# One in three of the streamed pieces of the selection stage moved from GpSimd to the vector engine

## Chip, cores and metric

One core of one Trainium2 chip. The metric is the device time of one execution in microseconds (us). The engines are named as the profile names them: PE (TensorE matmul), PEld (its weight load), DVE (VectorE), ACT (ScalarE), POOL (GpSimd) and SP (SyncE, which here only issues DMAs).

## What is computed

Four residual layers act on x of shape (8, 256, 256, 64): `x = x + layer(_gn(x))`, where `_gn` normalises each group of channels. The change lies in the last layer, a coherent semantic attention on the 512-feature view of the tensor. Here `_gn(x)` is the group norm (mean and 1/std for each image and channel), the feature rows hold 4096 points, of which 1024 are masked and 3072 are context:

```
cos  = einsum('bcm,bcn->bmn', msk_n, ctx_n)      # unit vectors, 1024 x 3072 for each image
maxc = cos.max(axis=-1);  amax = cos.argmax(axis=-1)
best = take_along_axis(ctx.transpose(0, 2, 1), amax[..., None], axis=1)
...                                               # a sequential scan blends best with its neighbours
out  = feats.at[:, :, mask_point_idx].set(gen)
```

The points occupy the first 64 of the 256 columns w of the picture. The other columns hold no points: there the layer gives back its own input, so the output is `x + _gn(x)`, which the kernel computes as `x * (1 + r) - r * mean` with r = 1/std.

## The kernel before

The program is a row of stages with a barrier between them; each is one function with hand-written programs for the five engines and semaphores between them. `select_points` (L1716) is the stage of the change. `point_rows` runs just before it and `coherent_scan` just after it.

**The selection.** For each of the 8 images b: POOL gathers 32 tiles of 128 point rows with indirect DMAs (`gather_rows`, L1801), one image ahead; ACT squares them, stores the context rows to DRAM (`cx`, L1845) and normalises them (L1854); PE transposes the tiles and DVE copies them out of PSUM (L1972). Then follow 8 search tiles. For each, PE makes 6 chunks of 128x512 cosines, ACT copies them from PSUM to one of two buffers `cos[:, i % 2]` (L1889), and DVE finds the greatest value and its place (`max` and `max_index`, L1977 and L1978; together one *search*). After the eighth DVE writes the indices `bi` (L1987, semaphore `s_bi`), and POOL gathers the best rows by them (L1832). ACT scales these in `scale_best`, which it does behind the second tile of the *next* image. ACT also does the squares of the next image behind tiles 2 to 4 and its normalising behind tiles 5 to 7; DVE does `norms` (four short instructions, L1958 to L1963) behind tile 4 and its own new work, if any, in the order in which the program lists it.

**The pointless columns.** They are cut into pieces of 128x1024 elements (512 KB). Of these the stage before does a few, and `select_points` streams 18 for each image (`NPC`) through a ring of four buffers `xt`. POOL's `stream(b)` first makes `s1` = 1 + r and `s0` = r * mean for the image (L1811, L1812, semaphore `s_sc`) and then does two `tensor_tensor` for each piece: times `s1` (L1817) and minus `s0` (L1819), both with both inputs in SBUF.

**The order of the ring.** SP issues, in this order and one after another: the load of piece n (L1785), which waits until the store of piece n-4 has landed, then the store of piece n-2 (L1780), which waits until that piece is computed. So a piece that is late holds back all later loads and stores.

**The order on POOL.** `gather_rows(0)`; then for each image b: `gather_rows(b + 1)`, `stream(b)`, wait for `s_bi` of image b, gather of the best rows of b. The last image has no `gather_rows`.

Of the kernel before, what the change touches and what calls it, by code (L numbers as in the profile page):

```python
# [10 lines left out]
ALU = mybir.AluOpType  # L11
# [15 lines left out]
PIECE = 16  # L27
# [45 lines left out]
def forward_modes(nc, tag, B, x, fa, fb, pair, eye, modes, nm, out_scale, split_rows):  # L73
# [4 lines left out]
    WG = W // G  # L78
    NPC = 8
    WP = WG // NPC  # L80
    CK = WP * C // 512
    NY = NPC * CK
    XB = 4
# [8 lines left out]
    with ExitStack() as ctx:  # L92
# [29 lines left out]
        s_pe, s_sp = m.sem("pe"), m.sem("spn")  # L122
        xv = x.rearrange("b (q p) (g t v) c -> b t p q g (v c)", p=P, g=G, t=NPC)
        fbank = [tz[0], tz[1], zp[0], zp[1]]
        with nc.Block() as block:

            @block.sync
            def _(sp):
# [5 lines left out]
                with sp.Fori(0, B) as b:  # L134
                    for i in range(NPC):
                        sp.wait_ge(s_y, b * NY + (i + 1) * CK)
                        sp.sem_inc(s_sp, 1)
                        sp.wait_ge(s_sq, b * NPC + (i + 1))
                        sp.sem_inc(s_sp, 1)
# [711 lines left out]
def spread(ap, dims):  # L851

    return bass.AP(ap.tensor, ap.offset, [[0, P]] + dims)
# [862 lines left out]
def select_points(nc, B, ft, mask_idx, ctx_idx, eye, cx, mnt, mbt, mx, x3, stats, out):  # L1716
# [9 lines left out]
    W0 = NPTS // C + EARLY * PIECE  # L1726
    NR = (W - W0) // PIECE
    NPC = 2 * NR
    with ExitStack() as ctx:
        m = Mem(nc, ctx, "sp")  # L1730
        rows = m.sb("rows", [P, 2, NT, H])
# [12 lines left out]
        xt = m.sb("xt", [P, 4, PIECE * C])  # L1744
        srow = m.sb("srow", [P, B, 2, C])
        s1, s0 = m.sb("s1", [P, PIECE, C]), m.sb("s0", [P, PIECE, C])
# [9 lines left out]
        s_sq, s_root, s_rn, s_nrm = m.sem("sq"), m.sem("root"), m.sem("rn"), m.sem("nrm")  # L1756
        s_t, s_te, s_c, s_ce = m.sem("t"), m.sem("te"), m.sem("c"), m.sem("ce")
        s_top, s_bi, s_ch, s_g2, s_mbs = m.sem("top"), m.sem("bi"), m.sem("ch"), m.sem("g2"), m.sem("mbs")
        s_row, s_sc, s_mul, s_out = m.sem("row"), m.sem("sc"), m.sem("mul"), m.sem("out")
        s_xt = [m.sem(f"xt{j}") for j in range(4)]  # L1760
        s_xs = [m.sem(f"xs{j}") for j in range(4)]

        def piece(t, n):

            b, r, i = n // NPC, n % NPC // NR, n % NR
            return t[b, r * P:(r + 1) * P, W0 + i * PIECE:W0 + (i + 1) * PIECE, :].rearrange("p w c -> p (w c)")

        ftf = ft.rearrange("b n h -> (b n) h")
        with nc.Block() as block:

            @block.sync
            def _(sp):
                sp.dma_start(idn[:, :], eye).then_inc(s_const, 16)
                sp.dma_start(idx0[:, 0:TM], mask_idx.rearrange("(t p) -> p t", p=P), allow_slow_non_contiguous=True).then_inc(s_const, 16)
                sp.dma_start(idx0[:, TM:NT], ctx_idx.rearrange("(t p) -> p t", p=P), allow_slow_non_contiguous=True).then_inc(s_const, 16)
                sp.dma_start(srow[:, :, :, :].rearrange("p b q c -> p (b q c)"), spread(stats, [[1, B * 2 * C]])).then_inc(s_row, 16)

                def store(n):
                    sp.wait_ge(s_out, n + 1)
                    sp.dma_start(piece(out, n), xt[:, n % 4, :]).then_inc(s_xs[n % 4], 16)  # L1780

                for n in range(B * NPC):
                    if n >= 4:
                        sp.wait_ge(s_xs[n % 4], 16 * (n // 4))
                    sp.dma_start(xt[:, n % 4, :], piece(x3, n)).then_inc(s_xt[n % 4], 16)  # L1785
                    if n >= 2:
                        store(n - 2)
                for n in range(B * NPC - 2, B * NPC):
                    store(n)
                for j in range(4):  # L1790
                    sp.wait_ge(s_xs[j], 16 * len(range(j, B * NPC, 4)))

            @block.gpsimd
            def _(pool):
                def gather_rows(b):
                    if b >= 2:
                        pool.wait_ge(s_cx[b % 2], 16 * (b // 2))
                        pool.wait_ge(s_nrm, b - 1)
                    pool.wait_ge(s_idx, b + 1)
                    for i in range(NT):  # L1800
                        pool.indirect_dma_start(rows[:, b % 2, i, :], None, ftf,  # L1801
                                                bass.IndirectOffsetOnAxis(ap=idx[:, i:i + 1], axis=0)).then_inc(s_g[b % 2][i // KC], 16)

                def stream(b):
                    r, mean = srow[:, b, 1, :], srow[:, b, 0, :]
                    rb = bass.AP(r.tensor, r.offset, [r.ap[0], [0, PIECE], r.ap[1]])
                    mb_ = bass.AP(mean.tensor, mean.offset, [mean.ap[0], [0, PIECE], mean.ap[1]])

                    if b:
                        pool.wait_ge(s_out, b * NPC)  # L1810
                    nc.gpsimd.tensor_scalar(s1[:, :, :], rb, 1.0, None, ALU.add)  # L1811
                    nc.gpsimd.tensor_tensor(s0[:, :, :], rb, mb_, ALU.mult).then_inc(s_sc, 1)  # L1812
                    pool.wait_ge(s_sc, b + 1)
                    for n in range(b * NPC, (b + 1) * NPC):
                        pool.wait_ge(s_xt[n % 4], 16 * (n // 4 + 1))
                        v = xt[:, n % 4, :]
                        nc.gpsimd.tensor_tensor(v, v, s1[:, :, :].rearrange("p w c -> p (w c)"), ALU.mult).then_inc(s_mul, 1)  # L1817
                        pool.wait_ge(s_mul, n + 1)
                        nc.gpsimd.tensor_tensor(v, v, s0[:, :, :].rearrange("p w c -> p (w c)"), ALU.subtract).then_inc(s_out, 1)  # L1819

                gather_rows(0)
                pool.wait_ge(s_row, 16)
                for b in range(B):
                    if b + 1 < B:
                        gather_rows(b + 1)
                    stream(b)
                    pool.wait_ge(s_bi, b + 1)
                    pool.wait_ge(s_cx[b % 2], 16 * (b // 2 + 1))
                    if b:
                        pool.wait_ge(s_bp, 4 * b)  # L1830
                    for i in range(TM):
                        pool.indirect_dma_start(best[:, i, :], None, cx[b],  # L1832
                                                bass.IndirectOffsetOnAxis(ap=bi[:, i:i + 1], axis=0)).then_inc(s_g2, 16)
# [115 lines left out]
            @block.vector  # L1949
            def _(dve):  # L1950
                ch = Chain(dve, s_ch)
                dve.wait_ge(s_const, 48)
                ch.step(nc.vector.tensor_copy(idxf[:, :], idx0[:, :]))
                nc.vector.tensor_copy(idx[:, :], idxf[:, :]).then_inc(s_idx, 1)  # L1954

                def norms(b):
                    dve.wait_ge(s_root, b + 1)
                    ch.step(nc.vector.tensor_scalar(rn[:, :], rn[:, :], CSA_EPS, None, ALU.add))  # L1958
                    nc.vector.reciprocal(rn[:, :], rn[:, :]).then_inc(s_rn, 1)
                    if b + 1 < B:  # L1960

                        ch.step(nc.vector.tensor_scalar(idxf[:, :], idxf[:, :], float(NPTS), None, ALU.add))
                        nc.vector.tensor_copy(idx[:, :], idxf[:, :]).then_inc(s_idx, 1)  # L1963

                norms(0)
                for b in range(B):
                    for i in range(NT // 2):
                        n = b * (NT // 2) + i
                        dve.wait_ge(s_t, n + 1)
                        if i == 0 and b:  # L1970
                            dve.wait_ge(s_mn, 16 * b)
                        nc.vector.tensor_copy(tc[:, :, 2 * i * P:(2 * i + 2) * P].rearrange("p r (q n) -> p q r n", q=2),  # L1972
                                              tp[n % 2][:, :, :, :]).then_inc(s_te, 1)
                    for i in range(TM):
                        n = b * TM + i
                        dve.wait_ge(s_ce, (n + 1) * NCH)
                        ch.step(nc.vector.max(top[:, i, :], cos[:, i % 2, :]))  # L1977
                        nc.vector.max_index(topi[:, i, :], top[:, i, :], cos[:, i % 2, :]).then_inc(s_top, 1)  # L1978
                        if i == SQ + 2 and b + 1 < B:
                            norms(b + 1)  # L1980
                    dve.wait_ge(s_top, (b + 1) * TM)
                    if b:
                        dve.wait_ge(s_mx, 16 * b)
                        dve.wait_ge(s_mbs, b)
                    ch.step(nc.vector.tensor_copy(bf[:, :], topi[:, :, 0]))
                    nc.vector.tensor_copy(mxo[:, :], top[:, :, 0])
                    nc.vector.tensor_copy(bi[:, :], bf[:, :]).then_inc(s_bi, 1)  # L1987
# [1144 lines left out]
```

## Time and profile before

| | |
|---|---|
| time before | 14682.73 us, median of 3 runs (14680.42 to 14685.68) |
| the profiled execution | 14687.5 us |
| its span, first to last instruction | 14685.3 us |
| busy in the span: PE / DVE / ACT / POOL | 10796.8 / 8873.9 / 6706.6 / 5138.0 us |
| `select_points`, by its first and the next stage's first DMA issue | 11450.8 to 12608.3 us |

The profile is of one execution; its rows give starts and durations in us from the first instruction. A line number is that of the kernel before. "Idle before" names what ended an engine's wait, as far as semaphore events show it. Shares of the whole span mix stages with different limits, so the rows below are taken from the stage of the change, and a few from other stages where the same kind of instruction runs under other conditions.

### The profile page before, as it was taken

What the parts mean: (1) busy time and instruction counts of PE and PEld (TensorE: products, weight loads), DVE (VectorE), ACT (ScalarE), POOL (GpSimd) and SP (SyncE); (2) the same over time, 40 slices, a digit from 0 to 9 for tenths busy, and PEclk for the clock granted to TensorE, in tenths of its full rate; (3) what the DMA queues carried; (4) which work ended last, traced back from release to release, by engine and by line L of the source; (5) the groups of instructions that cost most, each with busy time, mean ns of one, the idle gap of its engine ahead of it and who ended that gap; (6) DMA issues with size and microseconds to landing.
All of it is one profiled execution on the core that took longest, in us unless ns stands there. A gap on an engine that the chain in (4) does not pass through costs nothing. (4 is left out here: it accounts for less than half of the span.)

```text
span 14685.3 us, 297339 instructions
## 1 busy us (share of the span) xinstructions
PE 10796.8 (74%) x113226; PEld 7857.0 (54%) x113226; DVE 8873.9 (60%) x20267; ACT 6706.6 (46%) x10775; POOL 5138.0 (35%) x3844
## 2 busy tenths in 40 slices
PE   8655665999999999787787879986774677454432
PEld 3243222777777777666666668852322333344432
DVE  3213444777777777788888843322544545599992
ACT  5311222777777777566666632245233444222220
POOL 0002443656555655433333345520000689200001
PEclk9878887999999999999999989998787888555555
DMA  6686775111111111111111159997899666300008
GB/s 261 186 183 187 241 234 188 40 40 43 40 43 40 43 40 41 47 46 70 47 54 62 47 209 363 363 327 257 315 377 384 234 200 221 86 25 23 18 10 324
DMA packets 1298491, 2188.40 MB, mean 149 GB/s; under 512 B 116749, under 2 KB 951069, under 8 KB 1231781
## 3 DMA queue, kind: packets, MB, share of 16 engines
q1 hardware_dynamic: 878084, 1649.47, 33.9%
q10 hardware_dynamic: 398624, 463.54, 8.9%
q0 software_dynamic: 20608, 58.22, 1.4%
q8 instruction: 921, 15.09, 0.4%
q14 instruction: 254, 2.07, 0.0%
HBM read 1371.45 MB, written 799.58 MB: 148 GB/s over the span
## 5 line engine op out<-in xcount | busy, mean ns | idle before, releaser
L781 POOL TENSOR_TENSOR la_s<-la_s,la_mx 128x512 f32<-128x512 f32 x2048 | 2093.2, 1043 | 1458.0 <-DVE la_mx L740 1457.6
L820 ACT ACTIVATE la_et<-la_pt 128x512 f32<-128x512 f32 x2048 | 1120.2, 598 | 723.4 <-PE la_pt L652 723.4
L652 PE MATMUL la_pt<-la_idn,la_s 128*128 128x128 f32 x8192 | 1174.4, 289 | 214.8 <-POOL la_s L781 214.3
L740 DVE TENSOR_REDUCE la_mx<-la_s 128x16 f32<-128x1024 f32 x1024 | 1243.0, 1214 | 17.7
L732 DVE TENSOR_TENSOR la_s<-la_ps,la_post 128x2048 f32<-128x2048 f32 x512 | 1167.5, 2280 | 25.1 <-PE la_ps L638 25.1
L652 PEld LDWEIGHTS la_pt<-la_idn,la_s 128*128 128x128 f32 x8192 | 921.6, 146 | 328.1 <-issue 224.2
L2252 ACT ACTIVATE cs_sm<-cs_sm,cs_gq,cs_tt 8x1 f32<-8x1 f32 x1024 | 395.0, 386 | 1187.6 <-DVE cs_sm L2336 1187.6
L2135 PE MATMUL cs_tb<-cs_tt,cs_sel 8*128 8x16 f32 x2048 | 448.2, 370 | 652.6 <-DVE cs_tt L2334 652.6
L1439 PE MATMUL pj_pp<-pj_pw,pj_at 128*128 128x256 f32 x4096 | 927.5, 380 | 0.0
L956 PE MATMUL gm_xp<-gm_fws,gm_y 128*128 128x258 f32 x2048 | 561.6, 421 | 421.7 <-ACT gm_ri L1040 421.7
L1439 PEld LDWEIGHTS pj_pp<-pj_pw,pj_at 128*128 128x128 f32 x4096 | 759.3, 190 | 92.9
L1942 PE MATMUL sp_cp<-sp_tc 128*128 128x512 f32 x1536 | 694.8, 612 | 155.2 <-ACT sp_cos L1889 149.0
L2135 PEld LDWEIGHTS cs_tb<-cs_tt,cs_sel 8*128 8x128 f32 x2048 | 441.3, 327 | 675.1 <-DVE cs_tt L2334 637.8
L2410 POOL DMA_INDIRECT ft<-fp_g,fp_idx x64 | 62.1, 971 | 1992.0 <-DMA fp_g<-gen 1975.0
L1801 POOL DMA_INDIRECT sp_rows<-ft,sp_idx x256 | 243.0, 949 | 1332.8 <-DVE sp_idx L1954 1247.0
L2695 DVE SCALAR_TENSOR_TENSOR i_xo<-i_fp,i_xr 128x256 f32<-128x256 f32 x1024 | 379.2, 419 | 540.9 <-PE i_fp L2602 361.1
L956 PEld LDWEIGHTS gm_xp<-gm_fws,gm_y 128*128 128x128 f32 x2048 | 402.5, 206 | 563.7 <-issue 478.0
L1472 ACT ACTIVATE pj_at<-pj_tp 128x512 f32<-128x512 f32 x512 | 277.9, 594 | 862.7 <-PE pj_tp L1429 862.7
L1511 DVE TENSOR_TENSOR pj_o<-pj_pp,pj_xl 128x256 f32<-128x256 f32 x512 | 214.7, 419 | 755.2 <-PE pj_pp L1439 755.2
L1326 POOL TENSOR_TENSOR gm_sr<-gm_pc 128x512 f32<-128x512 f32 x64 | 70.0, 1093 | 1695.6 <-DVE gm_pc L1274 1695.6
L2717 POOL TENSOR_TENSOR i_acc<-i_acc,i_xo 128x4096 f32<-128x4096 f32 x56 | 496.3, 8863 | 411.9 <-DVE i_xo L2695 410.7
L751 DVE RECIPROCAL la_rc<-la_pt 128x32 f32<-128x32 f32 x512 | 183.1, 358 | 727.7 <-PE la_pt L661 727.7
(327 smaller groups left out, 27151.3 us busy)
## 6 DMA issues: line engine op xcount, KB each, us to landing
f_xt<-in_x SPq DMA_DIRECT2D x128, 1024.0 KB, 7.9
i_xr<-in_x SPq DMA_DIRECT2D x64, 2048.0 KB, 9.0
x<-pj_o SPq DMA_DIRECT2D x64, 2048.0 KB, 10.2
f_xt<-x SPq DMA_DIRECT2D x128, 1024.0 KB, 13.7
i_xr<-x SPq DMA_DIRECT2D x64, 2048.0 KB, 14.5
x<-i_xo ACTq DMA_DIRECT2D x64, 2048.0 KB, 14.6
sp_xt<-x SPq DMA_DIRECT2D x144, 512.0 KB, 4.6
out<-sp_xt SPq DMA_DIRECT2D x144, 512.0 KB, 2.9
```

Of the source, the lines that this page charges most:

```text
L652: last = nc.tensor.transpose(t_bank(S, i)[:, h, :], s[:, S % RS, i, h, :], idn[:, :])
L732: nc.vector.tensor_tensor(s[:, S % RS].rearrange("p t h i -> p h t i"), ps[:, :, :, :, :, :].rearrange("p h g e d i -> p h (g e) (d i)"), ...
L740: nc.vector.reduce_max(mx[:, S % RS, ts, :].rearrange("p t h -> p (t h)"), s[:, S % RS, ts].rearrange("p t h (d i) -> p (t h d) i", d=2), ...
L781: nc.gpsimd.tensor_tensor(sv, sv, mb, ALU.subtract).then_inc(s_sub, 1)
L820: nc.scalar.activation(et[:, k % RT].rearrange("p h n -> p (h n)"), t_bank(S, i)[:, :, :].rearrange("p h n -> p (h n)"), ACT.Exp).then_inc ...
L956: last = nc.tensor.matmul(xp[c % 2][q][:, :], y[:, c % 2, wh, q * P:(q + 1) * P], fws[:, q, wh, :], start=(wh == 0), stop=(wh == 1))
L1439: last = nc.tensor.matmul(pp[gg // 2][:, gg % 2, :, :].rearrange("p w d -> p (w d)"), at[:, q, s, g * P:(g + 1) * P], pw[:, s, :, :].rearr ...
L1942: last = nc.tensor.matmul(cp[n % 4][:, :], tc[:, r, i * P:(i + 1) * P], tc[:, r, c0:c0 + 512], start=(r == 0), stop=(r == 1))
L2135: last = nc.tensor.matmul(tb[:, c0:c0 + K], sel[:, b, :], tt[:, n * K:(n + 1) * K], start=True, stop=True)
L2252: nc.scalar.activation(sm[:, (s + 1) % 2, 7:8], sm[:, s % 2, 0:1], ACT.Sqrt, bias=gq[:, T % 2, s % P:s % P + 1], scale=tt[:, s:s + 1]).the ...
L2695: last = nc.vector.scalar_tensor_tensor(halves(xo, j, r, i)[:, s], f[:, s], 0.0, x[:, s], ALU.max, ALU.add)
L2717: nc.gpsimd.tensor_tensor(acc[:, :], acc[:, :], xo[:, wc % 2, :], ALU.add).then_inc(s_acc, 1)
```

## The change

Of every three pieces the third (n % 3 == 2) goes to DVE, the two others stay on POOL. DVE does its piece behind the search of a tile, six pieces for each image behind tiles 0 to 5. The pieces' buffers, their loads and stores and their order on SP stay as they are. The semaphores that count computed pieces are split in two, one for each engine, and POOL's wait before it makes `s1` and `s0` anew is for both.

```diff
+    SHARE = 3
+    ND = NPC // SHARE
...
+        s_mul, s_out = [m.sem(f"mul{j}") for j in range(2)], [m.sem(f"out{j}") for j in range(2)]
...
+        def by_vector(n):
+            return int(n % SHARE == SHARE - 1)
+
+        def finished(n):
+            d = (n + 1) // SHARE
+            return (n + 1 - d, d)[by_vector(n)]
...
                 def store(n):
-                    sp.wait_ge(s_out, n + 1)
+                    sp.wait_ge(s_out[by_vector(n)], finished(n))
...
                     if b:
-                        pool.wait_ge(s_out, b * NPC)
+                        pool.wait_ge(s_out[0], b * (NPC - ND))
+                        pool.wait_ge(s_out[1], b * ND)
...
                     for n in range(b * NPC, (b + 1) * NPC):
+                        if by_vector(n):
+                            continue
...
+                def stream(n):
+                    dve.wait_ge(s_sc, n // NPC + 1)
+                    dve.wait_ge(s_xt[n % 4], 16 * (n // 4 + 1))
+                    v = xt[:, n % 4, :]
+                    nc.vector.tensor_tensor(v, v, s1[:, :, :].rearrange("p w c -> p (w c)"), ALU.mult).then_inc(s_mul[1], 1)
+                    dve.wait_ge(s_mul[1], finished(n))
+                    nc.vector.tensor_tensor(v, v, s0[:, :, :].rearrange("p w c -> p (w c)"), ALU.subtract).then_inc(s_out[1], 1)
...
                         nc.vector.max_index(topi[:, i, :], top[:, i, :], cos[:, i % 2, :]).then_inc(s_top, 1)
+                        if i < ND:
+                            stream(b * NPC + i * SHARE + SHARE - 1)
                         if i == SQ + 2 and b + 1 < B:
                             norms(b + 1)
```

## Rows read from the trace of the kernel before

**Rows 1.** Busy time by engine in one image's stretch of the stage.

```profile
core 0: us, PE busy (x) PEld busy (x) DVE busy (x) ACT busy (x) POOL busy (x), PEclk, DMA share, GB/s
11917.00:12057.00 140.00, 102.43 (x272) 48.27 (x272) 71.05 (x47) 60.82 (x157) 126.53 (x78) 0.87 0.67 209
```

**Rows 2.** Timeline of POOL, one image: start, duration, line, idle before.

```profile
11635.30 1.04 POOL L1832 DMA_INDIRECT sp_best<-cx,sp_bi  x1 [0.15 <-issue]
...
11645.42 0.95 POOL L1801 DMA_INDIRECT sp_rows<-ft,sp_idx  x1 [0.30 <-issue]
...
11685.17 2.80 POOL L1811 TENSOR_SCALAR sp_s<-sp_srow 128x1024 f32<-128x1024 f32 x1
...
11690.37 2.35 POOL L1817 TENSOR_TENSOR sp_xt<-sp_xt,sp_s 128x1024 f32<-128x1024 f32 x1
...
11695.10 2.37 POOL L1817 TENSOR_TENSOR sp_xt<-sp_xt,sp_s 128x1024 f32<-128x1024 f32 x1
...
11775.95 1.02 POOL L1832 DMA_INDIRECT sp_best<-cx,sp_bi  x1
```

**Rows 3.** Timeline of POOL: first gather of best rows of the last two images.

```profile
12480.83 1.02 POOL L1832 DMA_INDIRECT sp_best<-cx,sp_bi  x1 [0.15 <-issue]
...
12581.37 1.03 POOL L1832 DMA_INDIRECT sp_best<-cx,sp_bi  x1 [0.15 <-issue]
```

**Rows 4.** Timeline of DVE: indices of an image, first search and a late one of the next.

```profile
12008.31 2.32 DVE L1987 CAST sp_bi<-sp_bf 128x8 int32<-128x8 f32 x1
...
12034.36 3.36 DVE L1977 MAX8 sp_top<-sp_cos 128x8 f32<-128x3072 f32 x1 [11.29 <-ACT sp_cos L1889]
...
12037.84 3.35 DVE L1978 FIND_INDEX8 sp_topi<-sp_top,sp_cos 128x8 uint32<-128x3072 f32 x1
...
12079.32 3.36 DVE L1977 MAX8 sp_top<-sp_cos 128x8 f32<-128x3072 f32 x1 [27.83 <-ACT sp_cos L1889]
```

**Rows 5.** Timeline of ACT in the same image.

```profile
12069.64 0.51 ACT L1862 ACTIVATE sp_best<-sp_best,sp_mxo 128x256 f32<-128x256 f32 x1 [25.01 <-DMA sp_best<-cx,sp_bi]
...
12115.31 0.37 ACTq L1845 DMA_DIRECT2D cx<-sp_rows  x1
...
12120.72 4.49 ACT L1854 ACTIVATE sp_nrm<-sp_rows,sp_rn 128x256 f32<-128x256 f32 x11
...
12131.02 4.48 ACT L1854 ACTIVATE sp_nrm<-sp_rows,sp_rn 128x256 f32<-128x256 f32 x11
```

**Rows 6.** Timelines of POOL (three rows), then DVE, in the global mixer stage.

```profile
7029.73 1.08 POOL L1330 TENSOR_TENSOR gm_dr<-gm_pc 128x508 f32<-128x508 f32 x1
...
7034.02 1.08 POOL L1339 TENSOR_TENSOR gm_di<-gm_pc 1x512 f32<-1x512 f32 x1
7035.07 2.07 POOL L1340 TENSOR_TENSOR gm_dr<-gm_ps 1x508 f32<-1x508 f32 x1
...
7034.10 2.10 DVE L1234 TENSOR_TENSOR gm_t<-gm_t 128x1032 f32<-128x1032 f32 x1
7036.24 2.00 DVE L1235 TENSOR_TENSOR gm_t<-gm_t 128x1032 f32<-128x1032 f32 x1
```

**Rows 7.** One line of `point_rows`, min/median/max ns: the same step on DVE, POOL idle.

```profile
L1695 DVE TENSOR_TENSOR pr_xt<-pr_xt,pr_s x48: 1217/1226/1227, 11183.2 to 11426.2; 128x1024 f32<-128x1024 f32 x48
```

**Rows 8.** DMA issues of the stage (KB, median us to landing); then landings at 12118:12123.

```profile
sp_xt<-x SPq DMA_DIRECT2D x144, 512.0 KB, 4.6
out<-sp_xt SPq DMA_DIRECT2D x144, 512.0 KB, 2.9
cx<-sp_rows ACTq DMA_DIRECT2D x8, 3072.0 KB, 18.1
...
DMA to landing us min/median/max: 6.9/7.4/8.9
```

**Rows 9.** Timeline of DVE: `norms` of the first image, POOL gathering.

```profile
11502.88 0.18 DVE L1958 TENSOR_SCALAR sp_rn<-sp_rn 128x32 f32<-128x32 f32 x1 [46.95 <-ACT sp_rn L1846]
...
11503.51 0.18 DVE L1963 CAST sp_idx<-sp_idxf 128x32 int32<-128x32 f32 x1
```

More of the change, by code:

```diff
@@ L1758, in select_points @@
         s_top, s_bi, s_ch, s_g2, s_mbs = m.sem("top"), m.sem("bi"), m.sem("ch"), m.sem("g2"), m.sem("mbs")
-        s_row, s_sc, s_mul, s_out = m.sem("row"), m.sem("sc"), m.sem("mul"), m.sem("out")
+        s_row, s_sc = m.sem("row"), m.sem("sc")
+        s_mul, s_out = [m.sem(f"mul{j}") for j in range(2)], [m.sem(f"out{j}") for j in range(2)]
         s_xt = [m.sem(f"xt{j}") for j in range(4)]
@@ L1766, in piece, with scales @@
             return t[b, r * P:(r + 1) * P, W0 + i * PIECE:W0 + (i + 1) * PIECE, :].rearrange("p w c -> p (w c)")
+        def by_vector(n):
[3 more added lines that the diff above has]
+            return (n + 1 - d, d)[by_vector(n)]
+        def scales(b):
+            r, mean = srow[:, b, 1, :], srow[:, b, 0, :]
+            return [bass.AP(v.tensor, v.offset, [v.ap[0], [0, PIECE], v.ap[1]]) for v in (r, mean)]
         ftf = ft.rearrange("b n h -> (b n) h")
@@ L1804, in stream @@
                 def stream(b):
-                    r, mean = srow[:, b, 1, :], srow[:, b, 0, :]
-                    rb = bass.AP(r.tensor, r.offset, [r.ap[0], [0, PIECE], r.ap[1]])
-                    mb_ = bass.AP(mean.tensor, mean.offset, [mean.ap[0], [0, PIECE], mean.ap[1]])
+                    rb, mb_ = scales(b)
                     if b:
-                        pool.wait_ge(s_out, b * NPC)
+                        pool.wait_ge(s_out[0], b * (NPC - ND))
+                        pool.wait_ge(s_out[1], b * ND)
                     nc.gpsimd.tensor_scalar(s1[:, :, :], rb, 1.0, None, ALU.add)
@@ L1814, in stream @@
                     for n in range(b * NPC, (b + 1) * NPC):
+                        if by_vector(n):
+                            continue
                         pool.wait_ge(s_xt[n % 4], 16 * (n // 4 + 1))
                         v = xt[:, n % 4, :]
-                        nc.gpsimd.tensor_tensor(v, v, s1[:, :, :].rearrange("p w c -> p (w c)"), ALU.mult).then_inc(s_mul, 1)
-                        pool.wait_ge(s_mul, n + 1)
-                        nc.gpsimd.tensor_tensor(v, v, s0[:, :, :].rearrange("p w c -> p (w c)"), ALU.subtract).then_inc(s_out, 1)
+                        nc.gpsimd.tensor_tensor(v, v, s1[:, :, :].rearrange("p w c -> p (w c)"), ALU.mult).then_inc(s_mul[0], 1)
+                        pool.wait_ge(s_mul[0], finished(n))
+                        nc.gpsimd.tensor_tensor(v, v, s0[:, :, :].rearrange("p w c -> p (w c)"), ALU.subtract).then_inc(s_out[0], 1)
                 gather_rows(0)
```

## The prediction

> **What bounds the kernel now.** The first view to read is the busy time by engine inside the stage, not over the whole span: in an image's 140 us POOL is busy for 126.5, and no other engine comes near [rows 1]. The rest of POOL's time are gaps of 0.3 us between gather instructions. The second view is POOL's timeline from one gather of best rows to the next [rows 2]: 10.1 us for the 8 gathers of best rows, 39.8 for the 32 gathers of the next image's rows, 5.2 for `s1` and `s0`, then 18 pieces at 4.73 and a little, 85.6 in all. Six such rounds take 12480.83 - 11635.30 = 845.5 us, 140.9 each, and the last, which has no gather of rows, 100.5 [rows 2, 3]. The third view are the waits of the others. ACT stands for 25.0 us behind the second tile until the best rows land, and DVE's third search then waits 27.8 us for ACT [rows 4, 5]. The indices are ready at 12010.6 (the end of the cast), some 47 us before POOL comes to use them. So POOL sets the round now and everything else has slack. What DVE has is not all slack, though: its program is in order, and that decides this case.
>
> **The change, part by part.** Call *best* the moment at which POOL starts the gathers of best rows, and S the start of its first piece. Best to S is 55.07 us [rows 2] and is not touched. Before, S to the next best is 140.9 - 55.07 = 85.85.
>
> *Removed from POOL:* 6 pieces of 4.73 for each image, 28.4 us. If POOL still set the round, it would fall to about 112 and the stage would gain some 200 us.
>
> *Added to DVE:* 12 `tensor_tensor` for each image, 1.226 each where POOL is idle [rows 7], 2.45 for a piece.
>
> *The port.* Both kinds of instruction read two SBUF operands. The nearest rows in which both engines run such instructions at once are in the global mixer [rows 6]: POOL's instruction ends at 7035.10, DVE's, which began at 7034.10, ends 1.10 us after that, POOL's next ends 0.94 us after DVE's, DVE's next again 1.10 after POOL's. Alone they take 1.23 and 1.08. So they take turns, and neither overlaps the other. A DVE turn is 1.10, a turn of POOL's on a piece 2.37 less the same 0.14, say 2.25. A piece of DVE's among POOL's then costs DVE up to 2.35 of waiting, 1.10, 2.25 and 1.10: 4.5 to 6.8 instead of 2.45, and it takes 2.2 from POOL. Lower bound: 2.45 and nothing from POOL, if the turns don't hold here. I take the turns, since the rows are of the same two instructions.
>
> *The added waits.* DVE waits for `s_sc` behind the search of tile 0. Before, that search ends about 30 us after the indices of the image before (12008.31 + 2.3 to 12041.2) [rows 4]. In the new order POOL will be waiting for these indices, so best follows them at once, and `s_sc` comes 55 us behind it. DVE therefore stands for some 25 us, and behind it stand the searches of tiles 1 to 7, by the two `cos` buffers ACT's copies from tile 3 on, and through them PE. Seven searches, the norms and the indices all lie behind S, and so the round is 55.1 + the time from S to the indices. The cover that hid all this before, POOL's 85.85, has gone down to some 57 to 71, so DVE sets the end.
>
> *From S to the indices, step by step* (S = 0). A search is 6.83 [rows 4]. A store lands 2.9 after its issue, a load 4.6 [rows 8]; the least that any one took is 2.6, which I keep as the lower end. Piece 2 lies in its buffer: both engines want the port, POOL 0 to 2.35, then DVE, POOL, DVE: 6.8. Tile 1 to 13.6. Piece 5 needs buffer 1: POOL ends piece 1 at 11.4, its store lands at 14.3, the load at 18.9, so **DVE waits 5.3 for the ring**; with the turns it is through at 25.6. Tile 2 to 32.4; piece 8 has landed (30.6); to 37.05. Tile 3 to 43.9; piece 11 to 48.5. Tile 4 to 55.3. Meanwhile ACT, which may copy tile 4 from 32.4, ends its squares and issues the `cx` store at about 44. In that store's first microseconds a 512 KB transfer lands in 6.9 to 8.9 [rows 5, 8]. So the store of piece 10 (44.1) lands at 51.0 and the load of piece 14 at 57.9: **a second ring wait, 2.6**. POOL has run dry by then, and the piece takes 2.45, to 60.35. Norms 0.8 [rows 9], tile 5 to 68.0, piece 17 to 73.0, tile 6 to 79.9. ACT: its first normalising starts with the norms at 60.9, and a tile's copies and a third of the normalising take 10.3 [rows 5], so tile 7's copies end at 81.5. Tile 7 to 88.4, the indices at 89.0.
>
> The sum: 89.1 against 85.85 is +3.25 us for each of the images 0 to 6 (image 0 has the same S; its tile 0 search is done about then), +23. The last round: no gather of rows, so S is 15.3 behind best and DVE stands for nothing; from the indices 23.8 to the first search [rows 4], 8 searches of 6.83 and 6 pieces of about 4.5 give 105.4, against 100.5: +5. Together **+28 us**, from 14687.5 to 14716 for an execution like the profiled one. The median lies 4.8 lower: 14711.
>
> *Edits that cost nothing:* the split semaphores change no time; POOL's wait for both before `s1` is met long before, since DVE's last piece lies two searches ahead of the indices. SP issues the same 36 transfers for each image in the same order. The stage behind starts at the same distance from the last best gather.
>
> *A rule of the skill.* The Trainium skill, page "Perfetto Trace Analysis", section "Optimizing Scalar/DVE Operations", says that the two engines share an SBUF read port and that moving work between them might not help. It speaks against the change. By it alone POOL would keep what the turns leave, a round of some 126, and the stage would gain about 100 us; by the rows the turns are only a part, and the waiting in order behind S is what takes the gain.
>
> **Rivals.** *No turns:* DVE's pieces run beside POOL's at 2.45. The same steps then give 19.5 behind piece 5, 29.3 behind 8, 39.0 behind 11, with `cx` at 38 piece 14 at 52.6 to 55.1, the indices at 83.6. That is -2.15 for each image, +3 at the end: -12, 14671. Against it speak rows 6. This is the way to "not slower", and it decides from S to the indices under 85.
>
> *No turns and a ring that is never late:* then DVE's own work counts alone, 68 from S to the indices (ACT's two spans of 10.3 behind tile 4 included): -17.6 for each of 7, -120, about 14563. The profile has nothing for a ring without delay: a buffer comes back only by a store and a load.
>
> *The ring under the `cx` store is worse:* with 8.9 for each transfer from 44 on, piece 14 lands at 61.9 and piece 17 at 74, the indices at 97.4: +11.6 for each image, +5: +86, 14769. For it: before, the store met a ring with POOL alone at 4.73 a piece, all behind one another, and SP had to wait there too; now it meets DVE's pieces. Against it: the rows are 6.9 to 8.9 in the first 5 us only.
>
> *It doesn't do what it says:* excluded as far as counts can, since 96 pieces stay on POOL and 48 go to DVE by the loops.
>
> **How the numbers follow.** The forecast's case (turns, ring at the medians) gets 0.55; its own range is +5 to +50, by loads between 2.6 and 6.9 and by which engine gets the port first (2.35 either way at S). The bad ring gets 0.20, no turns 0.17, the gain 0.08. The range of 14660 to 14775 takes in the first three and leaves out the gain and what lies above. About 0.2% (29 us) is what a measurement of this kernel can tell from no change. The forecast lies just under that line, so its case gives half to either side. Slower by more: 0.20 + 0.27 = 0.47; within: 0.28 + 0.17 = 0.45; faster by more: 0.08.
>
> **What would show it.** In the profile of the changed kernel POOL's line L1817 counts 96 and not 144, and POOL waits for the indices before each gather of best rows, for up to 18 us. From one best to the next 144, best to S still 55. Behind the search of tile 0 DVE stands for about 25 us until `s_sc`. DVE's two instructions of a piece last 1.2 to 3.5 each and POOL's beside them up to 3.5. DVE waits for loads at pieces 5 and 14. ACT no longer waits for the best rows. The prediction is wrong if best follows the indices with a delay (POOL is the bound again), if the DVE instructions last 1.23 beside POOL's (no turns), or if the waits for loads are none or beyond 5 us each.

## The result, and the profile after

The changed kernel took 14730.66 us (median of 9 runs, 14722.22 to 14748.9), the kernel before 14684.71 on the same chip: a ratio of 1.0033, 95% interval 1.0023 to 1.0042, so 46 us slower. The profiled execution took 14730.66, its span is 14728.9. The medians of this document are of the chip's usual state: one execution of the last run below and two of the run without the wait for POOL's rows, at 15475 us and more, are left out.

POOL did 96 pieces instead of 144 and lost its place as the bound, and the rounds became longer. The first view is the timeline of POOL, first gather of best rows of three images (start, duration, line; in brackets the idle time before it and what ended it):

```profile
12074.36 1.03 POOL L1848 DMA_INDIRECT sp_best<-cx,sp_bi  x1 [18.00 <-DVE sp_bi L2014]
...
12221.52 1.02 POOL L1848 DMA_INDIRECT sp_best<-cx,sp_bi  x1 [18.58 <-DVE sp_bi L2014]
...
12625.88 1.02 POOL L1848 DMA_INDIRECT sp_best<-cx,sp_bi  x1 [16.56 <-DVE sp_bi L2014]
```

In [rows 2, 3] these gathers followed at once on the last piece. Now POOL has done its pieces and waits 18 us for the indices. From image 0 to image 6 (11630.59 to 12514.18) a round is 147.3 us and was 140.9; the last is 111.7 and was 100.5. From the stage's first gather (11447.13, before 11456.21) to its last first gather of best rows the stage takes 53.6 us more; the earlier stages were 9 us shorter in this profile.

The waits inside the stage (engine, tile and line that waits, what for; us in total, times, longest):

```profile
DVE sp_xt L1986 <- POOL sp_s L1826: 151.3, 7, 25.2
POOL sp_best L1848 <- DVE sp_bi L2014: 145.5, 8, 19.9
DVE sp_xt L1986 <- DMA sp_xt<-x: 104.7, 21, 10.1
...
ACT sp_best L1878 <- DMA sp_best<-cx,sp_bi: 23.3, 1, 23.3
```

DVE stands up to 25 us for the scale rows, seven times, and 13 us an image for loads. ACT's wait for the best rows [rows 5] is left once, 23.3 us; before it was there seven times, 171.9 us in all.

The timeline of DVE in one image, its work on pieces and the indices only (S, POOL's first piece, is at 12129.33):

```profile
12129.28 1.23 DVE L1986 TENSOR_TENSOR sp_xt<-sp_xt,sp_s 128x1024 f32<-128x1024 f32 x1 [24.74 <-POOL sp_s L1826]
12130.54 3.25 DVE L1988 TENSOR_TENSOR sp_xt<-sp_xt,sp_s 128x1024 f32<-128x1024 f32 x1
...
12150.58 1.77 DVE L1986 TENSOR_TENSOR sp_xt<-sp_xt,sp_s 128x1024 f32<-128x1024 f32 x1 [10.06 <-DMA sp_xt<-x]
...
12188.76 1.88 DVE L1986 TENSOR_TENSOR sp_xt<-sp_xt,sp_s 128x1024 f32<-128x1024 f32 x1 [5.75 <-DMA sp_xt<-x]
...
12221.08 0.16 DVE L2014 CAST sp_bi<-sp_bf 128x8 int32<-128x8 f32 x1
```

Here are all three things at once: the wait for the scale rows, instructions of 3.25 where alone they take 1.23, and waits for the loads of pieces 5 and 14. From S to the indices are 91.9 us. Before, POOL itself needed 85.85 from S to the next gather of best rows, which hid any path of DVE's shorter than that; now DVE's path is 6.1 us longer than that cover was.

By line, of the whole stage (busy us, mean ns of one, idle before):

```profile
L1835 POOL TENSOR_TENSOR sp_xt<-sp_xt,sp_s 128x1024 f32<-128x1024 f32 x96 | 254.3, 2649 | 7.5
L1833 POOL TENSOR_TENSOR sp_xt<-sp_xt,sp_s 128x1024 f32<-128x1024 f32 x96 | 245.7, 2559 | 88.5 <-DMA sp_xt<-x 87.6
...
L1988 DVE TENSOR_TENSOR sp_xt<-sp_xt,sp_s 128x1024 f32<-128x1024 f32 x48 | 126.0, 2626 | 1.7
```

The counts are as the change says, and both engines' instructions are longer than alone (2.35 on POOL [rows 2], 1.23 on DVE [rows 7]).

### The profile page after: what moved, and what is told of

Same layout as the page of the kernel before. It is cut to its first block and busy times, and to the rows that moved or that the text cites. A ratio compares the mean times of both kernels' runs of the same rounds, so it can differ in the third digit from the quotient of the medians.

```text
span 14728.9 us, 297394 instructions
## 1 busy us (share of the span) xinstructions
PE 10807.7 (73%) x113226; PEld 7858.8 (53%) x113226; DVE 9034.9 (61%) x20363; ACT 6706.8 (46%) x10775; POOL 4964.0 (34%) x3748
## 5 line engine op out<-in xcount | busy, mean ns | idle before, releaser
L1958 PEld LDWEIGHTS sp_cp<-sp_tc 128*128 128x128 f32 x1536 | 306.0, 202 | 625.5 <-issue 371.2
## 6 DMA issues: line engine op xcount, KB each, us to landing
x<-pj_o SPq DMA_DIRECT2D x64, 2048.0 KB, 10.1
i_xr<-x SPq DMA_DIRECT2D x64, 2048.0 KB, 14.3
```

The costliest lines, as they stand in the source:

```text
L1958: last = nc.tensor.matmul(cp[n % 4][:, :], tc[:, r, i * P:(i + 1) * P], tc[:, r, c0:c0 + 512], start=(r == 0), stop=(r == 1))
```

## The experiments

Three suspects stand behind the result: the **wait** for the scale rows at DVE's first piece, the **turns** of the two engines, and the **ring** of four buffers. The first four runs take away one thing each. For each run the table has the median time, the ratio to the kernel before in the same batch, and, from its profile, the mean of the six rounds between the best gathers of images 0 to 6 and the last round.

| run | us | ratio, 95% interval | round | last |
|---|---|---|---|---|
| before | 14684.71 | 1 | 140.9 | 100.5 |
| the change | 14730.66 | 1.0033 [1.0023, 1.0042] | 147.3 | 111.7 |
| no wait for POOL's rows | 14721.53 | 1.0027 [1.0017, 1.0038] | 143.3 | 111.0 |
| no turns | 14705.32 | 1.0013 [1.0003, 1.0022] | 141.7 | 110.2 |
| DVE's waits alone | 14686.22 | 1.0000 [0.9990, 1.0011] | 140.0 | 105.5 |
| two thirds on POOL, the rest nowhere | 14544.36 | 0.9905 [0.9885, 0.9925] | 122.1 | 83.1 |
| late places | 14632.31 | 0.9964 [0.9950, 0.9978] | 127.5 | 112.5 |
| late places, no turns | 14614.15 | 0.9958 [0.9944, 0.9972] | 124.8 | 110.6 |
| six buffers | 14697.70 | 1.0009 [0.9999, 1.0019] | 141.8 | 105.9 |
| late, no turns, six buffers | 14580.73 | 0.9931 [0.9915, 0.9948] | 119.7 | 116.7 |
| no turns, no wait | 14703.28 | 1.0013 [1.0004, 1.0023] | 143.2 | 108.1 |
| no turns, no wait, six buffers | 14622.70 | 0.9957 [0.9941, 0.9973] | 131.3 | 108.0 |

**No wait for POOL's rows.** `wide` is the row of the image, broadcast over a piece.

```diff
+        d = m.sb("d", [P, 2, B, C])
...
+                ch.step(nc.vector.tensor_scalar(d[:, 1, :, :], srow[:, :, 1, :], 1.0, None, ALU.add))
+                ch.step(nc.vector.tensor_tensor(d[:, 0, :, :], srow[:, :, 1, :], srow[:, :, 0, :], ALU.mult))
...
-                    dve.wait_ge(s_sc, n // NPC + 1)
...
+                    nc.vector.tensor_tensor(v, v, wide(1, n), ALU.mult).then_inc(s_mul[1], 1)
```

> The changed kernel, but DVE makes its own row of 1 + r and of r * mean for all images once, at the start of the stage, and reads them repeated 16 times, so that its pieces no longer wait for POOL's s_sc. In the changed kernel that wait is 24.7 us for each image. Theory (DVE's program order and the ring of buffers): the wait is not what costs. Piece 5 cannot come before POOL has finished piece 1, so DVE, having done piece 2 and tile 1 early, then stands at piece 5 until about 20 us after POOL's first piece (S), as now (21.2). POOL is rid of two turns in its first piece, so some 2 us for each image come back: round 145 instead of 147.2, time 14710 to 14730. Rival (the wait for s_sc is the cost): 25 us for each image come back until POOL sets the round at about 126, time about 14580.

14722, 9 us less than the change; the two intervals overlap, so this difference is not clear of the noise. Its DVE timeline, pieces 2 and 5 of the image whose S is at about 12126:

```profile
12100.84 1.21 DVE L1993 TENSOR_TENSOR sp_xt<-sp_xt,sp_d 128x1024 f32<-128x1024 f32 x1
12102.08 1.22 DVE L1995 TENSOR_TENSOR sp_xt<-sp_xt,sp_d 128x1024 f32<-128x1024 f32 x1
12144.28 3.40 DVE L1993 TENSOR_TENSOR sp_xt<-sp_xt,sp_d 128x1024 f32<-128x1024 f32 x1 [33.06 <-DMA sp_xt<-x]
```

Piece 2 is done 41 us before piece 5 starts, ahead of S and without any wait; and then DVE stands 33 us for a load. The wait has only gone one piece further. (The table's round is from the shortest execution of this kernel, 14714 us in span.) The rival, that this wait is the price (14580), falls.

**No turns.** The scale rows lie in PSUM, so that a DVE instruction has one operand in SBUF. For the space one of the two PSUM buffers of the best rows is given up; the wait stays.

```diff
+        bp = m.ps("bp", [P, 512])
+        d = m.ps("d", [P, 4, 2, C])
...
+                    v = xt[:, n % 4, :].rearrange("p (w c) -> p w c", c=C)
+                    nc.vector.tensor_tensor(v, v, wide(1, n), ALU.mult).then_inc(s_mul[1], 1)
```

> The changed kernel, but the two scale rows that DVE reads lie in PSUM (a bank taken from the second buffer for the transposed best rows), so that its tensor_tensor has one input in SBUF and not two; the wait for s_sc stays. Theory: the instructions no longer take turns with POOL's, 1.2 us each on DVE and 2.35 on POOL, 4.5 for a piece of DVE's becomes 2.45 at four of its six pieces; the ring takes half of it back, since pieces 5 and 14 still wait for loads. From POOL's first piece to the indices 86 to 88 instead of 92, round 141 to 143, time 14690 to 14705, no faster than the kernel before. Rival (the turns at the port are the whole loss): POOL sets the round at 113 to 126, time 14500 to 14590. Rival (no turns there at all): no change, 14730.

14705, the upper end of what the theory said. The lines of this run:

```profile
L1840 POOL TENSOR_TENSOR sp_xt<-sp_xt,sp_s 128x1024 f32<-128x1024 f32 x96 | 226.3, 2357 | 7.5
...
L1993 DVE TENSOR_TENSOR sp_xt<-sp_xt,sp_d 128x1024 f32<-128x1024 f32 x48 | 58.6, 1220 | 1.6
```

DVE's instruction is back at 1.22 and POOL's at 2.36, side by side. It is not the broadcast row that does this: the run before read the same broadcast from SBUF, and there DVE's second instruction of a piece took 2.55 in the mean. So the turns are a matter of the second SBUF operand, and they cost 5.6 us a round and 25 us in all. The Trainium skill, page "SBUF — State Buffer", section "Who interferes with whom", says that a VectorE instruction with two SBUF inputs contends with a GpSimd instruction that reads SBUF. The two profiles agree: the second instruction of a piece took 2.63 on DVE and 2.65 on POOL in the mean where DVE's had two SBUF inputs, 1.22 and 2.36 where it had one.

**DVE's waits alone.** DVE's two instructions on a piece are replaced by one of a single column:

```diff
-                    nc.vector.tensor_tensor(v, v, s1[:, :, :].rearrange("p w c -> p (w c)"), ALU.mult).then_inc(s_mul[1], 1)
-                    dve.wait_ge(s_mul[1], finished(n))
-                    nc.vector.tensor_tensor(v, v, s0[:, :, :].rearrange("p w c -> p (w c)"), ALU.subtract).then_inc(s_out[1], 1)
+                    nc.vector.memset(xt[:, n % 4, 0:1], 0.0).then_inc(s_out[1], 1)
```

> The changed kernel without DVE's arithmetic on its pieces: DVE keeps every wait and its place in the order, and instead of the two tensor_tensor writes one column. Left out: a third of the pieces of this stage is not computed. Theory: the waits alone hold most of the loss. POOL has its 12 pieces without turns, but DVE still stands for s_sc, for piece 5 until about 19 us after POOL's first piece and for piece 14 under the cx store; from POOL's first piece to the indices 83 to 86, round 138 to 141, time 14670 to 14690: hardly better than the kernel before, though neither engine computes those pieces. Rival (the arithmetic or the turns are the cost): POOL sets the round at 113, time about 14490.

14686: the time of the kernel before, although POOL has a third less to do and DVE no arithmetic on pieces. POOL still waits for the indices, in every image:

```profile
POOL sp_best L1848 <- DVE sp_bi L2011: 138.8, 8, 18.0
```

In one image S to the indices is 85.1 (12107.67 to 12192.81). The waits alone eat the whole 28 us of an image that were taken from POOL. That 85.1 comes so near to POOL's old 85.85 is chance: nothing ties them.

**Two thirds on POOL, the rest nowhere.** SP stores the third pieces as soon as they are loaded, and DVE has nothing to do with them:

```diff
+                    if by_vector(n):
+                        sp.wait_ge(s_xt[n % 4], 16 * (n // 4 + 1))
...
-                        if i < ND:
-                            stream(b * NPC + i * SHARE + SHARE - 1)
```

> The changed kernel with the third pieces computed by nobody: DVE does not touch them, SP stores each as soon as it has landed. Left out: a third of the pieces of this stage. It is the removal alone. Both theories: POOL sets the round again at 140.9 - 28.4 = 112.5, if the chain of searches allows it (from the best rows to the next indices some 92 + 13 = 105); time about 14685 - 7 x 28 - 25 = 14460 to 14500. If the round is clearly above 113, another chain than POOL's bounds there and the room for any such change is smaller than thought.

The gain is there, 142 us, but less than I said: the round is 122.1, not 112.5. POOL is the bound again (its best gathers follow at once), with a wait:

```profile
L1837 POOL TENSOR_TENSOR sp_xt<-sp_xt,sp_s 128x1024 f32<-128x1024 f32 x96 | 226.3, 2357 | 7.5
L1835 POOL TENSOR_TENSOR sp_xt<-sp_xt,sp_s 128x1024 f32<-128x1024 f32 x96 | 226.1, 2355 | 76.3 <-DMA sp_xt<-x 75.4
```

Its instructions take what they took, 12 pieces of 4.72 in an image; the 75.4 us of waiting for loads are 9.4 an image. Before, POOL waited 0.9 us for loads in the whole stage. So a ring of four keeps up with 18 pieces in 85 us but not in 57. I take 122 as about the floor for this split with four buffers and this order on SP, since no place for DVE's pieces gives their buffers back sooner than this run did; that is argued, and no run shows it by itself.

**Late places.** DVE does its pieces 2, 5 and 8 behind tiles 4 to 6, 11 behind the indices, 14 and 17 behind tiles 0 and 1 of the next image:

```diff
-                        if i < ND:
-                            stream(b * NPC + i * SHARE + SHARE - 1)
+                        if i < 2 and b:
+                            stream((b - 1) * NPC + (i + 4) * SHARE + SHARE - 1)
                         if i == SQ + 2 and b + 1 < B:
                             norms(b + 1)
+                        if 4 <= i < 7:
+                            stream(b * NPC + (i - 4) * SHARE + SHARE - 1)
...
+                    stream(b * NPC + 3 * SHARE + SHARE - 1)
...
```

> All of the change stays, both engines do the same pieces with the same instructions, but DVE's six pieces of an image stand at other places of its program: pieces 2, 5 and 8 behind the searches of tiles 4, 5 and 6 (behind the norms), piece 11 right behind the indices, pieces 14 and 17 behind the searches of tiles 0 and 1 of the next image (of the last image at its end). My theory, that DVE's waiting in order for the scale rows takes the gain: seven searches no longer stand behind that wait, the indices are ready when POOL comes to them, POOL sets the round again. From the run in which POOL kept two of three pieces and nobody computed the third, a round is then 122, and the port turns that the changed kernel shows (0.5 us on a piece of POOL's, 12 pieces) make it 125 to 130: 14580 to 14620 us. Rival, the port turns eat the gain: they are the same here, so 14715 to 14735. Rival, pieces so late hold up the ring (SP stores in order): POOL waits for loads for over 25 us of an image, 14650 or more.

The same work at other places: 14632, 98 us less than the change. POOL's best gathers again follow at once on its last piece, and DVE has no wait for the scale rows left:

```profile
12410.54 2.34 POOL L1835 TENSOR_TENSOR sp_xt<-sp_xt,sp_s 128x1024 f32<-128x1024 f32 x1
12413.04 1.02 POOL L1848 DMA_INDIRECT sp_best<-cx,sp_bi  x1 [0.16 <-issue]
```

The round, 127.5, is where I said. The time is 12 us above my range, because I had left out both ends. In image 0 no DVE search runs ahead, and POOL stands for the ring; in the last image, where no gather of rows gives DVE time, POOL stands before it can make new scale rows until DVE has used the old ones for the late pieces of the image before:

```profile
11605.60 2.37 POOL L1833 TENSOR_TENSOR sp_xt<-sp_xt,sp_s 128x1024 f32<-128x1024 f32 x1 [38.19 <-DMA sp_xt<-x]
...
12443.58 2.77 POOL L1825 TENSOR_SCALAR sp_s<-sp_srow 128x1024 f32<-128x1024 f32 x1 [20.67 <-DVE sp_xt L1988]
```

So image 0's best gather comes 193.3 us behind the stage's first gather and not 179.1, and the last round is 12 us longer than before. Six rounds give back 81; these two take 26.

```profile
L1835 POOL TENSOR_TENSOR sp_xt<-sp_xt,sp_s 128x1024 f32<-128x1024 f32 x96 | 244.1, 2543 | 7.5
L1833 POOL TENSOR_TENSOR sp_xt<-sp_xt,sp_s 128x1024 f32<-128x1024 f32 x96 | 237.3, 2472 | 118.6 <-DMA sp_xt<-x 117.5
...
L1988 DVE TENSOR_TENSOR sp_xt<-sp_xt,sp_s 128x1024 f32<-128x1024 f32 x48 | 101.4, 2113 | 1.7
```

The turns are still there, though fewer: a piece costs POOL 5.02 us, against 5.21 in the change and 4.71 without turns, and the gain is there all the same, so the first rival falls. The second holds only at the ends: of POOL's 117.5 us of waiting for loads 39.9 are in image 0 and 15.2 in the last, and the six images between have 10.4 each in the mean.

**Late places, no turns.** The late places on top of the scale rows in PSUM, and without the wait for POOL's:

```diff
-                    dve.wait_ge(s_sc, n // NPC + 1)
```

> The same late places, and DVE reads its scale rows from PSUM, made by itself, so that it has no wait for POOL's rows and one SBUF operand only. My theory: no turns, POOL's instructions last 2.35 again, and the round is that of the run in which nobody computed the third pieces, 122: 14540 to 14570 us. Rival, turns don't count once POOL bounds: as the late places alone, within 10 us. Rival, late pieces hold up the ring: over 14600.

14614 and a round of 124.8, 2.7 above the floor of 122.1, but 44 us above my range, for the most part by both ends again (a wait of 37.4 for a load in image 0, a last round of 110.6). What came is the second rival, late pieces that hold up the ring: POOL waits 129.6 us for loads, in the mean 12.1 in each of the six images between the ends, where the run without any third pieces had 9.4. Against the late places alone 18 us are gained, less than the 25 that the same edit gave where DVE was the bound.

**Six buffers.** The changed kernel, the ring longer and nothing else:

```diff
+        xt = m.sb("xt", [P, 6, PIECE * C])
...
+                    if n >= 6:
+                        sp.wait_ge(s_xs[n % 6], 16 * (n // 6))
+                    sp.dma_start(xt[:, n % 6, :], piece(x3, n)).then_inc(s_xt[n % 6], 16)
+                    if n >= 4:
+                        store(n - 4)
```

> The changed kernel with six buffers in the ring, and SP stores a piece four loads later, not two; nothing else. My theory: DVE's waits for loads behind S (about 16 us of an image) go, since pieces up to 5 lie in buffers at S and later ones are fetched further ahead; the wait for the scale rows of 25 us stays, and with it the order. From S to the indices: piece 2 done 4.5, tile 1 11.2, piece 5 16, tile 2 23, piece 8 28, tile 3 35, piece 11 40, tile 4 47, piece 14 52, the norms, tile 5 59.5, ACT's copies of tile 7 end at 75 to 77, the indices at 82 to 84 and not 92: rounds of 137 to 139, 14650 to 14675 us. Rival, the ring is no part of it: 14715 to 14735. Rival, only the ring keeps DVE late: 14600 or less.

33 us less than the change, but not the 56 to 81 of the theory. Its waits:

```profile
POOL sp_best L1848 <- DVE sp_bi L2014: 159.6, 8, 21.2
...
DVE sp_xt L1986 <- POOL sp_s L1826: 150.2, 7, 25.1
...
DVE sp_xt L1986 <- DMA sp_xt<-x: 11.4, 15, 1.5
```

DVE's waits for loads fell from 104.7 to 11.4 us, 11.7 an image, but S to the indices only by 6.0 (85.9, 12120.26 to 12206.18 of one image). Half the cleared time went to turns, since POOL no longer runs dry while DVE works: DVE's two instructions take 1.87 and 2.87 in the mean (1.77 and 2.63 in the change), 2 us for six pieces, and even the norms are hit:

```profile
L1974 DVE TENSOR_SCALAR sp_rn<-sp_rn 128x32 f32<-128x32 f32 x8 | 16.3, 2044 | 46.9 <-ACT sp_rn L1862 46.9
L1978 DVE TENSOR_SCALAR sp_idxf<-sp_idxf 128x32 f32<-128x32 f32 x7 | 12.1, 1733 | 0.0
```

Steps that took 0.17 and 0.12 in the change's profile (12191.82 and 12192.30 of the image above) take 2.04 and 1.73: 3.5 us more. The kernel before had this too: 1.25 and 1.78 in the mean of the same two steps, where POOL was busy beside them.

**Late, no turns, six buffers.** All remedies together, the late places without turns and

```diff
+        xt = m.sb("xt", [P, 6, PIECE * C])
```

> Late places, scale rows in PSUM, and six buffers. My theory: with no wait in order, no turns and no wait for loads POOL alone sets the round, 55 from the best gathers to its first piece and 12 pieces of 4.72, so 112 to 115: 14465 to 14510 us. Rival, the transfers themselves are the limit under POOL (36 of 512 KB in an image): the round stays near 122, 14540 to 14570.

14581, 103 us faster than the kernel before (ratio 0.9931) and 150 faster than the change: the best of the runs, but short of the theory. The round of 119.7 lies between the 112 to 115 and the rival's 122, and the ends put the time above both ranges: POOL waits 29.6 us for one load in image 0 and, in the last, 25.7 for DVE's pieces of the image before (a last round of 116.7). POOL still waits 93.3 us for loads. One image between the ends shows where: 2.66, 1.49 and 0.70 us. SP stores in order, and in that image the store of piece 2 waits until DVE has done it behind tile 4 and the norms, 9.7 us behind the store before (SP's issues at 12062.12 and 12071.82). The late place has its own price.

**No turns, no wait; and with six buffers.** These put the suspects together at the places of the change. The edit is that of the run without turns and, in both,

```diff
-                    dve.wait_ge(s_sc, n // NPC + 1)
```

The second has the ring of six as well.

> The changed kernel with the places as they are; DVE reads scale rows of its own from PSUM (no turns, as in the run without turns, 14705) and does not wait for POOL's rows. Ring of four. My theory: two waits lie behind one another, and the later one decides. DVE does piece 2 and the search of tile 1 ahead of S, but the load of piece 5 is issued only when POOL's piece 1 of the image is stored, and lands 19 to 20 us behind S as before; from there all is as it was: 14695 to 14715 us. Rival, the wait for the scale rows has a price of its own: the searches move ahead by some 11 us, 14620 to 14640.

> The same with six buffers, a store four loads later. No wait for the scale rows, no turns, and loads further ahead; the places are still those of the change. My theory: only with all three gone the gain comes. SP issues the load of piece 5 behind the store of POOL's first piece, so DVE still stands until about 10 us behind S, then goes through: tile 2 to S + 19, piece 14 done at S + 40, the norms, and 29 us of ACT's copies and the last search: the indices at S + 70, rounds of 124 to 127, 14570 to 14605 us. Rival, the effects simply add (25 for the turns, 33 for the ring, 7 for the wait): 14665 us. Rival, something else holds the searches behind S: over 14680.

The first: 14703, no less than without turns alone. DVE has no wait for POOL any more, and in exchange

```profile
DVE sp_xt L1990 <- DMA sp_xt<-x: 279.1, 32, 32.7
```

The second: 14623, a round of 131.3. With the wait and the turns gone the ring is worth 12 us a round, twice the 5.4 that it was worth alone; so the effects do not simply add (14665). It is 18 us above my range, though. In one image S is at 12064.91 and piece 5 starts 9.5 behind it, as expected, but it is not the last wait:

```profile
12074.42 1.22 DVE L1990 TENSOR_TENSOR sp_xt<-sp_xt,sp_d 128x1024 f32<-128x1024 f32 x1 [23.10 <-DMA sp_xt<-x]
...
12085.65 1.22 DVE L1990 TENSOR_TENSOR sp_xt<-sp_xt,sp_d 128x1024 f32<-128x1024 f32 x1 [2.02 <-DMA sp_xt<-x]
...
12108.21 1.22 DVE L1990 TENSOR_TENSOR sp_xt<-sp_xt,sp_d 128x1024 f32<-128x1024 f32 x1 [3.48 <-DMA sp_xt<-x]
```

The 23.10 was foreseen; the 2.02 and 3.48 behind it (and two of 0.7) I had at nothing, and norms of 2.4 at about 1. The indices come at S + 77 and not 70.

## Why the prediction was right

The mechanism, its place and its sign were as forecast; the size was +28 forecast, +46 measured. By one of the signs that I had named for it, the prediction was wrong: waits for loads beyond 5 us each. They were 10.1 and 5.75 in the image below (and 5.3 was already in my own steps). One image of the changed kernel against the steps (us behind S):

| step | forecast | measured |
|---|---|---|
| piece 2 done | 6.8 | 4.5 |
| piece 5 starts, wait before it | 18.9, 5.3 | 21.3, 10.1 |
| piece 8 done | 37.1 | 35.6 |
| tile 4 done | 55.3 | 53.7 |
| piece 14 starts, wait before it | 57.9, 2.6 | 59.4, 5.75 |
| ACT's normalising starts | 60.9 | 63.1 |
| tile 7's copies end | 81.5 | 84.6 |
| indices | 89.0 | 91.9 |

**Held.** POOL's 96 counts; best to S 55.0, with a round of 147.3 where I said 144; DVE's stand of 25 us for `s_sc`; POOL's wait for the indices (18 said, 16.6 to 19.9 seen); the turns, with DVE's instructions at 1.2 to 3.4 and POOL's up to 3.4; waits for loads at pieces 5 and 14; ACT free of the best rows. The run of the waits alone and the run of the late places bear out the central step: work behind a wait in order on DVE, not work on POOL, sets the round. The three runs that take away one suspect each (the wait for the rows, the turns, two more buffers) show that taking away one alone does not give the gain: none of the three is faster than the kernel before.

**Port at S.** I gave POOL the first turn; DVE had it and was through 2.3 us earlier. That gain did not last: DVE waits for piece 5 anyway, and stood there so much longer.

**The landing of loads, mis-sized.** I took the median of before, 4.6 [rows 8]. SP issued the load of piece 5 at S + 14.4 (forecast 14.3), and DVE could start 6.9 later:

```profile
12141.13 0.43 SPq L1800 DMA_DIRECT2D sp_xt<-x  x1
12141.61 0.79 SPq L1795 DMA_DIRECT2D out<-sp_xt  x1
12143.69 0.33 SPq L1800 DMA_DIRECT2D sp_xt<-x  x1
```

The last of these is that load; a load and a store had been issued just ahead of it. By the medians of this stage the stores took 4.1 instead of 2.9 and the loads 4.9 instead of 4.6. I had copied a landing time from a ring that had slack into one that had none.

In this image the late load of piece 5 did not itself make the indices late. POOL stood for loads too (0.95 and 1.75 us before its pieces 4 and 6), so piece 5 lost only 0.5 us to a turn, and tile 4 was done 1.6 us ahead of the forecast. But those waits made POOL end piece 10 1.8 us late. The store of piece 10 and the load of piece 14 then took 7.3 and 6.2 us (forecast 6.9 each), piece 14 started 1.5 us late, and a turn that I had left out made it 0.7 longer. That the `cx` store itself makes the second wait longer was not tried by a run.

**The tail.** From ACT's first normalising to the indices were 28.8, against 28.1 forecast: the first tile's copies took 11.1 and not 10.3. With the 1.5 and 0.7 of piece 14 that makes the 2.9 by which the indices came late in this image.

**The ends.** I had no wait for the ring in the last image. DVE waited 6.59 at piece 5 and 1.60 at piece 8; the last round came to 111.7 and not 105.4. The profiled execution is 43 us longer than the one before, about 16 more than forecast: 20 are 7 images at 2.8 for the terms above, 6 are this end, and the stages that the change does not touch were 10 shorter, 9 of them ahead of this one. So in the stage alone the loss was 53.6, nearly twice the 28; that this execution came nearer was luck.

**Rivals.** *No turns* was excluded by the rows of the mixer, rightly: the run without turns shows what they cost. But its price was wrong too. I had 14671 for it and the run gave 14705, since its loads were late in the same way (DVE waited 135.5 us for them). *A bad ring under `cx`* was nearer than I allowed: the measured time lies between forecast and that rival. The rule of the Trainium skill, page "Perfetto Trace Analysis", section "Optimizing Scalar/DVE Operations" (a shared port, so that moving work may not help), named a real cost, 5.6 us of a round, but it is not what took the gain: with the turns gone and the waits kept the kernel is still slower than before, and with the pieces moved and most of the turns kept it is 0.4% faster, at the round of 127.5 against the 126 that I had worked out for turns alone.

## What to carry to other kernels

Work handed to an engine that has slack is put into that engine's order, and its waits are handed over with it: ask, for each moved step, what it waits for, what stands behind it in the program, and when that is due. The same twelve instructions cost 46 us at one place and gained 51 at another. When two waits lie behind one another, taking away the first shows little (here 9 us, with a wait of 33 us at the next piece); take away both before you acquit either. And landing times of a buffer ring with slack are no price for the same ring when it sets the pace.

## What the runs showed of the hardware

- DVE's `tensor_tensor` with two SBUF operands and POOL's take whole turns (3.25 and 3.2 to 3.4 instead of 1.23 and 2.35), and this hits tiny instructions too: a `tensor_scalar` of 128x32 took 2.04 in the mean beside a busy POOL (the run with six buffers), 0.18 beside gathers [rows 9]. `max` kept its 3.35, and with one operand in PSUM `tensor_tensor` kept its 1.22.
- Transfers of 512 KB landed later where they followed one another more closely: with 12 pieces of POOL's and no DVE work on pieces at all, 18 pieces in some 66 us instead of 85, loads landed in 5.0 and stores in 4.6 us in the median (4.6 and 2.9 before), and POOL waited 9.4 us an image for loads.
